# Routed expert tiles of a vision tower taken two at a time, with six weight buffers and the first four tiles' weights requested during routing

## The chip, the cores and the metric

One core of a Trainium2 chip runs the whole program. The metric is the time of one execution on the device in microseconds (us); of several executions the median counts. The engines are TensorE (PE, with its weight loads PEld), VectorE (DVE), ScalarE (ACT), GpSimd (POOL) and SyncE (SP, here an issuer of DMAs).

## What is computed

Sixty-four images become 1024 tokens of 192 values. Two layers follow: attention and a soft mixture of experts, then attention and a routed mixture of experts. The change lies in the last part, which is

```python
def _L1_ffn_ref(x, Wg, bg, Wge, bge, W1, b1, W2, b2):   # G=4 groups, E=8 experts each, D=192, M=768
    xf = x.reshape(-1, D)
    comb = _combine_weights(xf, Wg, bg, Wge, bge)       # best 2 groups, in each the best 2 experts
    h = jax.nn.gelu(jnp.einsum('nd,edm->nem', xf, W1) + b1, approximate=False)
    y = jnp.einsum('nem,emd->ned', h, W2) + b2
    out = jnp.einsum('ne,ned->nd', comb, y)
...
h = h + _L1_ffn_ref(_layernorm(h, axis=-1), L1_ffn_Wg, L1_ffn_bg, ...)
```

All arithmetic is fp32. Each token goes to 4 of 32 experts.

## The kernel before

`route` works out, for each of the 4096 (token, expert) pairs, a place in a list sorted by expert and padded so that every run of 128 places, a **tile**, has a single expert. There are `MOE_TILES` = 63 tiles. The tables are `rt.slot` (the token of every place) and `rt.expert` (the expert of every tile). The order in `route` is written out by hand: DVE computes the places, then one-hot matrices in four quarters; POOL multiplies them (L1325), PE sums them (L1350), and DVE turns the sums into `rt.slot` (L1448 to L1456) and last copies `rt.expert` (L1458). SP writes the normalised tokens to memory and waits for nothing but their landing.

`expert_tiles` then runs tiles 0 to 62. For tile t:

- POOL gathers the 128 token rows from memory into `x`, a ring of nine buffers (`gather`, L1717).
- SP reads the tile's expert from `rt.expert` and loads its two weight matrices, 576 KB each, into `w1` and `w2`, rings of three (`load`, L1521 and L1524). It waits until the hidden product (`hid_ready`), and then the output product (`y_ready`), of tile t-3 have left those buffers.
- PE transposes the 128 rows into the one bank `xp` (`transpose_x`, L1553); DVE copies them to `xT`, a ring of three, and picks the gate values (`leave_x`).
- PE makes the hidden values in `up`. The 192 input channels are split in 128 and 64. Six products over 128 rows (L1565) start the six chunks of 128 hidden values, and six products over 64 rows (L1568) end them. The even chunks' 64 rows lie on partitions 0 to 63 and the odd ones' on 64 to 127, so that two of them run in the array side by side. An fp32 product is two records in the trace, so the rows show 12 for six.
- ACT adds the bias and applies gelu (L1630) into `H`, a ring of three, as `hp` in PSUM is.
- PE makes the output in `down`: six products over 128 rows with 192 columns each (L1580) into the one bank `yp`. DVE scales them by the gate into `y`, a ring of three (`leave_y`, L1663), and POOL adds them to one of three sums in memory (`scatter`, L1729). `leave_y` of tile t waits until the scatter of tile t-3 has landed.

All engines follow the order that `tile` gives. On PE it is: transpose tile t+1, `up(t)`, `down(t-1)`. `program` writes out the first nine tiles and the last nine, and runs the 45 between in a loop of five rounds (`Fori`). The last two tiles aren't scattered; their rows are put in place by products (L1606). At the end SP reads the three sums back, DVE adds them, and SP writes the result.

## Time and profile before

| | us |
|---|---|
| median of 3 executions | 1133.21 |
| lowest, highest | 1131.98, 1136.58 |
| the profiled execution | 1137.21 |
| its span in the trace | 1135.4 |
| mean granted TensorE clock | 0.945 of full speed |

The page gives each engine's busy time, the span in 40 slices, the chain of work that ended last, and the costliest groups of instructions. PE is busy for 1011.5 us of the span (89%), ACT for 669.8, DVE for 396.8 and POOL for 256.9. The expert tiles run from 825 to 1123 us, so the last 300 us of the span are the part to read. PE's lengths in the timeline overlap, since a product starts before the one ahead of it has left the array; the distance between starts is what counts.

### The profile page before, as it was taken

What the parts mean: (1) busy time and instruction counts of PE and PEld (TensorE: products, weight loads), DVE (VectorE), ACT (ScalarE), POOL (GpSimd) and SP (SyncE); (2) the same over time, 40 slices, a digit from 0 to 9 for tenths busy, and PEclk for the clock granted to TensorE, in tenths of its full rate; (3) what the DMA queues carried; (4) which work ended last, traced back from release to release, by engine and by line L of the source; (5) the groups of instructions that cost most, each with busy time, mean ns of one, the idle gap of its engine ahead of it and who ended that gap; (6) DMA issues with size and microseconds to landing.
All of it is one profiled execution on the core that took longest, in us unless ns stands there. A gap on an engine that the chain in (4) does not pass through costs nothing. (4 is left out here: it accounts for less than half of the span.)

```text
span 1135.4 us, 22122 instructions
## 1 busy us (share of the span) xinstructions
PE 1011.5 (89%) x7464; PEld 659.8 (58%) x7464; DVE 396.8 (35%) x1021; ACT 669.8 (59%) x1227; POOL 256.9 (23%) x256
## 2 busy tenths in 40 slices
PE   8878779879999999999999998875179999999997
PEld 8345445433445444444444455454169999999996
DVE  2655968550011111111111114766932222222233
ACT  0475968579888888888888862361033343333431
POOL 0111333230000000000000000200455555555541
PEclk9889969889999999999999999897579999999999
DMA  9000008979555555445545501004089999999997
GB/s 345 15 1 1 1 30 334 317 301 175 124 126 115 124 125 117 113 112 116 127 101 124 123 1 47 0 1 134 1 316 311 312 306 307 314 306 305 315 287 198
DMA packets 76118, 185.27 MB, mean 163 GB/s; under 512 B 15889, under 2 KB 34545, under 8 KB 75769
## 3 DMA queue, kind: packets, MB, share of 16 engines
q1 hardware_dynamic: 63788, 169.45, 49.5%
q0 software_dynamic: 11808, 14.39, 6.4%
q8 instruction: 53, 0.87, 0.4%
q14 instruction: 37, 0.30, 0.1%
q10 hardware_dynamic: 432, 0.26, 0.1%
HBM read 148.37 MB, written 35.69 MB: 162 GB/s over the span
## 5 line engine op out<-in xcount | busy, mean ns | idle before, releaser
L1182 ACT ACTIVATE sle_H<-sle_hp 128x1024 f32<-128x1024 f32 x384 | 367.5, 1024 | 58.9 <-PE sle_hp L1119 58.8
L1630 ACT ACTIVATE ext_H<-ext_hp,ext_bias 128x128 f32<-128x128 f32 x378 | 104.2, 375 | 171.7 <-issue 154.7
L1136 PE MATMUL sle_up<-sle_H,sle_cw 128*32 128x512 f32 (+1 forms) x2048 | 192.6, 494 | 0.0
L1580 PE MATMUL ext_yp<-ext_w,ext_H 128*128 128x192 f32 x756 | 139.7, 335 | 0.6 <-issue 0.6
L1197 DVE STREAM_TRANSPOSE sle_UT<-sle_up 128x256 f32<-128x256 f32 x64 | 37.3, 583 | 292.9 <-PE sle_up L1136 292.9
L1580 PEld LDWEIGHTS ext_yp<-ext_w,ext_H 128*128 128x128 f32 x756 | 121.1, 190 | 8.4 <-issue 0.9
L1119 PE MATMUL sle_hp<-keep_G,keep_dT 99*128 99x512 bf16 (+1 forms) x512 | 102.4, 334 | 11.7 <-PEq L897 6.8
L1104 POOL COPY sle_cw<-keep_CT 128x128 f32 (+1 forms) x64 | 18.7, 293 | 394.2 <-PE sle_up L1136 394.1
L1136 PEld LDWEIGHTS sle_up<-sle_H,sle_cw 128*32 128x32 f32 x2048 | 53.7, 109 | 87.2 <-issue 73.8
L1119 PE MATMUL sle_hp<-sle_G,sle_dT 99*128 99x512 bf16 (+1 forms) x512 | 100.0, 327 | 1.1 <-ACT sle_H L1182 1.1
L1565 PE MATMUL ext_hp<-ext_xT,ext_w 128*128 128x128 f32 x756 | 95.9, 277 | 0.0
L1119 PEld LDWEIGHTS sle_hp<-keep_G,keep_dT 99*128 99x128 bf16 x512 | 45.0, 99 | 82.3 <-ACT sle_H L1182 32.8
L1565 PEld LDWEIGHTS ext_hp<-ext_xT,ext_w 128*128 128x128 f32 x756 | 90.7, 194 | 0.0
L1119 PEld LDWEIGHTS sle_hp<-sle_G,sle_dT 99*128 99x128 bf16 x512 | 44.5, 98 | 69.4 <-ACT sle_H L1182 30.3
L1641 DVE COPY ext_yi<-rmoe_slot 128x1 uint32 (+1 forms) x63 | 9.7, 154 | 204.1 <-PE ext_yp L1580 204.1
L1729 POOL DMA_INDIRECT sum<-ext_y,ext_yi x40 | 63.6, 1590 | 68.5 <-DVE ext_gate L1654 32.7
L1145 PE MATMUL sle_up<-keep_w,sle_UT 128*128 128x192 f32 x384 | 67.3, 326 | 0.8 <-DVE sle_UT L1197 0.8
L1717 POOL DMA_INDIRECT ext_x<-xn,ext_xi x63 | 62.0, 985 | 25.1 <-issue 18.3
L1145 PEld LDWEIGHTS sle_up<-keep_w,sle_UT 128*128 128x128 f32 x384 | 61.7, 190 | 2.1 <-DVE sle_UT L1197 1.7
L1568 PE MATMUL ext_hp<-ext_xT,ext_w 64*128 64x128 f32 x756 | 59.1, 289 | 0.0
L979 PE MATMUL hid_gps<-pre_w,vit_xnT 128*128 128x384 f32 x128 | 48.0, 520 | 5.4 <-DVE hid_rest L1022 5.4
L1568 PEld LDWEIGHTS ext_hp<-ext_xT,ext_w 64*128 64x128 f32 x756 | 47.1, 187 | 7.6
(272 smaller groups left out, 1206.9 us busy)
## 6 DMA issues: line engine op xcount, KB each, us to landing
ext_w<-W SPq DMA_DIRECT2D x126, 576.0 KB, 5.4
pieces<-hid_gp SPq DMA_DIRECT2D x16, 1152.0 KB, 4.6
keep_G<-pieces SPq DMA_DIRECT2D x32, 288.0 KB, 3.9
sle_G<-pieces SPq DMA_DIRECT2D x32, 288.0 KB, 3.8
pieces<-hid_gp SPq DMA_DIRECT2D x8, 768.0 KB, 5.3
keep_G<-pieces SPq DMA_DIRECT2D x32, 192.0 KB, 3.8
sle_G<-pieces SPq DMA_DIRECT2D x32, 192.0 KB, 3.8
keep_CT<-xT SPq DMA_DIRECT2D x6, 512.0 KB, 6.8
```

What stands on the lines that cost most here:

```text
L979: pe.matmul(gps[(STEPS * i + e) % 4][:, half, 0:HALF], g.wideT[:, 0, tokens], g.w1[:, e - 1, half * HALF:(half + 1) * HALF], start=True, s ...
L1119: mm = pe.matmul(hp[k % DEEP][:, j, off:off + width], dT[b][:, c * P:(c + 1) * P], G[b][:, (c // 2) * HID + at:(c // 2) * HID + at + width ...
L1136: mm = pe.matmul(to[32 * e:32 * e + 32], cw[:, p, 2 * e + grp, :], H[:, p, h:h + width], start=(p == 0 and grp == 0), stop=(p == 1 and grp ...
L1145: mm = pe.matmul(yps, UT[:, par, b, :], g.w2[:, b, :], start=(b == blocks[0]), stop=(b == blocks[-1]))
L1182: act.activation(H[:, p, WIDTH * k:WIDTH * (k + 1)], hp[k % DEEP][:].rearrange("p a c -> p (a c)"), ACT.Gelu_apprx_tanh).then_inc(gelu_don ...
L1197: dve.transpose(UT[:, par, at // 32:(at + width) // 32, 32 * j:32 * j + 32], src.rearrange("p (b c) -> p b c", c=32)).then_inc(ut_done[ban ...
L1565: pe.matmul(hp[q][:, c % 2, (c // 2) * P:(c // 2 + 1) * P], w1[:, q, c, :], xT[:, q, 0, :], start=(c < 2), stop=False)
L1568: mm = pe.matmul(hp[q][:, c % 2, (c // 2) * P:(c // 2 + 1) * P], w1[rows, q, HC + c // 2, :], xT[rows, q, 1, :], start=False, stop=(c >= H ...
L1580: mm = pe.matmul(yp[:, 0:D], H[:, q, c, :], w2[:, q, c, :], start=(c == 0), stop=(c == HC - 1))
L1630: act.activation(H[:, q, c, :], hp[q][:, c % 2, (c // 2) * P:(c // 2 + 1) * P], ACT.Gelu, bias=bias[:, q, c:c + 1]).then_inc(gelu_done, 1)
L1717: pool.indirect_dma_start(out=x[:, p, :], out_offset=None, in_=xn_dram, in_offset=bass.IndirectOffsetOnAxis(ap=xi[p][:], axis=0)).then_inc ...
L1729: pool.indirect_dma_start(out=sums[q], out_offset=bass.IndirectOffsetOnAxis(ap=yi[q][:], axis=0), in_=y[:, q, :], in_offset=None, compute_ ...
```

## The change

1. **Pairs.** `up` is cut in `heads` (the six 128-row products) and `tails` (the six 64-row products). Tile 0 runs by itself; tiles 1 to 62 run in 31 pairs. For a pair t, t+1 PE does: transpose t+1, `heads(t)`, `down(t-2)`, transpose t+2, `heads(t+1)`, `down(t-1)`, `tails(t)`, `tails(t+1)`. DVE and POOL follow that order.
2. **Six weight buffers.** `w1` and `w2` have six buffers (`DEPTH`), and the loads of tile t wait for tile t-6. The buffers and their semaphores now live in `routed_moe`, and are called `rmoe_w` in the listing. The other rings keep their depth, except the gate values (`GATES`), which have six.
3. **Weights during routing.** `rt.expert` is computed before the one-hot matrices instead of last, and SP requests the weights of tiles 0 to 3 (`AHEAD`) inside `route`. In `expert_tiles` SP writes `out` first, and then loads tile 4 and on.
4. **Straight code.** No engine has a loop any more; all 63 tiles are written out. The `turn` increments on POOL go away.

PE, in the second and third tile of the expert stage. Before:

```order
L1553 MATMUL ext_xp<-vit_ident,ext_x 128x128 x2
L1565 MATMUL ext_hp<-ext_xT,ext_w 128x128 x6
L1568 MATMUL ext_hp<-ext_xT,ext_w 128x128 x6
L1580 MATMUL ext_yp<-ext_w,ext_H 128x192 x6
L1553 MATMUL ext_xp<-vit_ident,ext_x 128x128 x2
L1565 MATMUL ext_hp<-ext_xT,ext_w 128x128 x6
L1568 MATMUL ext_hp<-ext_xT,ext_w 128x128 x6
L1580 MATMUL ext_yp<-ext_w,ext_H 128x192 x6
```

PE, one pair of the changed kernel (L1546 transposes, L1558 `heads`, L1576 `down`, L1564 `tails`):

```order
L1546 MATMUL ext_xp<-vit_ident,ext_x 128x128 x2
L1558 MATMUL ext_hp<-ext_xT,rmoe_w 128x128 x6
L1576 MATMUL ext_yp<-rmoe_w,ext_H 128x192 x6
L1546 MATMUL ext_xp<-vit_ident,ext_x 128x128 x2
L1558 MATMUL ext_hp<-ext_xT,rmoe_w 128x128 x6
L1576 MATMUL ext_yp<-rmoe_w,ext_H 128x192 x6
L1564 MATMUL ext_hp<-ext_xT,rmoe_w 128x128 x12
```

The same 64-row products stand in one run of twelve for two tiles, where two runs of six stood, each between products over 128 rows.

SP, at the end of routing. Before:

```order
L1312 DMA sum<-rte_zero 128x9x192 x2
L1314 DMA xn<-rmoe_gate 128x8x4
L1252 UNCONDITIONAL_BRANCH
L1514 UNCONDITIONAL_BRANCH
L1517 TENSOR_LOAD rmoe_expert
L1517 ISA x2
L1521 ISA
L1521 DMA ext_w<-W 128x1152
L1524 DMA ext_w<-W 128x1152
```

SP in the changed kernel, the first of four such loads:

```order
L1312 DMA sum<-rte_zero 128x9x192 x2
L1314 DMA xn<-rmoe_gate 128x8x4
L1469 TENSOR_LOAD rmoe_expert
L1469 ISA x2
L1472 ISA
L1472 DMA rmoe_w<-W 128x1152
L1475 DMA rmoe_w<-W 128x1152
```

The loads have moved ahead of the branch that ends `route`.

```diff
+            sp.wait_ge(rt.expert_ready, 1)
+            for t in range(rt.AHEAD):
+                load_weights(sp, a, rt, t)
...
+            dve.wait_ge(owner_out, 1)
+            dve.tensor_scalar(rt.expert[:], ps_cnt[0:1, P:P + MOE_TILES], float(EXPERTS - 1), None, ALU.min).then_inc(rt.expert_ready, 1)
...
-            dve.wait_ge(owner_out, 1)
-            dve.tensor_scalar(rt.expert[:], ps_cnt[0:1, P:P + MOE_TILES], float(EXPERTS - 1), None, ALU.min).then_inc(slot_done, 1)
-            dve.wait_ge(slot_done, 2)
+            dve.wait_ge(slot_done, 1)
+            dve.wait_ge(rt.expert_ready, 1)
+
+
+def load_weights(sp, a, rt, t):
+
+    q = t % rt.DEPTH
+    e = sp.value_load(rt.expert[0:1, t:t + 1], min_val=0, max_val=EXPERTS - 1)
+    if t >= rt.DEPTH:
+        sp.wait_ge(rt.hid_ready, t - rt.DEPTH + 1)
+    sp.dma_start(rt.w1[:, q].rearrange("p c n -> p (c n)"), a["W1"][bass.ds(e, 1)].rearrange("o p n -> (o p) n")).then_inc(rt.w1_in[q], 16)
+    if t >= rt.DEPTH:
+        sp.wait_ge(rt.y_ready, t - rt.DEPTH + 1)
+    sp.dma_start(rt.w2[:, q], a["W2"][bass.ds(e, 1)].rearrange("o p c n -> (o p) c n")).then_inc(rt.w2_in[q], 16)
...
-    DEEP, BODY, PLACED = 3, 9, 2
-    ROUNDS = MOE_TILES // BODY
+    RING, XS, GATES, PLACED = 3, 9, 6, 2
+    LAST = MOE_TILES - 1
+    PAIRED = range(1, LAST, 2)
...
+            sp.wait_ge(h_done, TILES // 2)
+            sp.dma_start(out[0:TOKENS].rearrange("(i p) d -> p i d", p=P), g.h[:]).then_inc(first_out, 16)
+            sp.dma_start(out[TOKENS:TOKENS + P], g.h[:, 0, :]).then_inc(first_out, 16)
+            for t in range(rt.AHEAD, MOE_TILES):
+                load_weights(sp, a, rt, t)
...
+            def heads(t):
+                q, w = t % RING, t % rt.DEPTH
+                pe.wait_ge(rt.w1_in[w], 16 * (t // rt.DEPTH) + 16)
                 pe.wait_ge(xT_done, t + 1)
-                if first and p == 1:
+                if t == 1:
                     pe.wait_ge(h_done, TILES // 2)
-                if not (first and p < DEEP):
-                    pe.wait_ge(gelu_done, HC * (t - DEEP + 1))
+                if t >= RING:
...
+            def tails(t):
...
-            def tile(t, p, r, first, last):
-                if first and p == 0:
-                    transpose_x(0, 0, 0)
-                if not (last and p == BODY - 1):
-                    transpose_x(t + 1, (p + 1) % BODY, r + (p + 1) // BODY)
-                up(t, p, r, first)
-                if not (first and p == 0):
-                    down(t - 1, (p - 1) % BODY, r + (p - 1) // BODY)
...
-            program(pe, tile)
-            down(MOE_TILES - 1, BODY - 1, ROUNDS - 1)
+            transpose_x(0)
+            transpose_x(1)
+            heads(0)
+            tails(0)
+            for t in PAIRED:
+                transpose_x(t + 1)
+                heads(t)
+                if t >= 2:
+                    down(t - 2)
+                if t + 2 < MOE_TILES:
+                    transpose_x(t + 2)
+                heads(t + 1)
+                down(t - 1)
+                tails(t)
+                tails(t + 1)
+            down(LAST - 1)
+            down(LAST)
...
+            def gather_index(t):
+                if t >= XS:
+                    dve.wait_ge(x_in[t % XS], 16 * (t // XS))
+                dve.tensor_copy(xi[t % XS][:], rt.slot[:, 0, t:t + 1]).then_inc(xi_ready, 1)
...
+                if t + XS < MOE_TILES:
+                    gather_index(t + XS)
...
-            program(dve, tile)
-            leave_y(MOE_TILES - 1, BODY - 1, ROUNDS - 1, False)
+            leave_x(0)
+            leave_x(1)
+            for t in PAIRED:
+                leave_x(t + 1)
+                if t >= 2:
+                    leave_y(t - 2)
+                if t + 2 < MOE_TILES:
+                    leave_x(t + 2)
+                leave_y(t - 1)
+                if t == LAST - 9:
+                    place_rows()
+                if t in (LAST - 7, LAST - 5):
+                    place_tile((t - LAST + 7) // 2)
+            leave_y(LAST - 1)
+            leave_y(LAST)
...
+            for t in range(XS + 2):
+                gather(t)
+            for t in PAIRED:
+                if t + 1 + XS < MOE_TILES:
+                    gather(t + 1 + XS)
+                if t >= 2:
+                    scatter(t - 2)
+                if t + 2 + XS < MOE_TILES:
+                    gather(t + 2 + XS)
+                if t - 1 < MOE_TILES - PLACED:
+                    scatter(t - 1)
+            pool.wait_ge(y_out[0], 16 * (MOE_TILES // RING))
...
+        rt.DEPTH, rt.AHEAD = 6, 4
...
+        rt.w1 = s.sb("w1", [P, rt.DEPTH, HC + HC // 2, P])
+        rt.w2 = s.sb("w2", [P, rt.DEPTH, HC, D])
+        rt.w1_in, rt.w2_in = ([s.sem(f"{n}{i}") for i in range(rt.DEPTH)] for n in ("w1_in", "w2_in"))
+        rt.expert_ready, rt.hid_ready, rt.y_ready = (s.sem(n) for n in ("expert_ready", "hid_ready", "y_ready"))
```

## Rows read from the trace of the kernel before

**Rows 1.** The page, costliest groups: shapes, count, busy us, mean ns, idle before:
```profile
L1565 PE MATMUL ext_hp<-ext_xT,ext_w 128*128 128x128 f32 x756 | 95.9, 277 | 0.0
```

**Rows 2.** Stretches: length, busy time of each engine, PEclk, DMA share, GB/s:
```profile
860.00:1088.68 228.68, 228.68 (x1902) 215.51 (x1901) 58.68 (x298) 87.56 (x350) 126.75 (x98) 1.00 0.99 309
```

**Rows 3.** Timeline of PE, one tile: start, length in us (merged instructions):
```profile
942.33 1.50 PE L1565 MATMUL ext_hp<-ext_xT,ext_w 128*128 128x128 f32 x12
943.76 0.94 PE L1568 MATMUL ext_hp<-ext_xT,ext_w 64*128 64x128 f32 x12
944.63 2.22 PE L1580 MATMUL ext_yp<-ext_w,ext_H 128*128 128x192 f32 x12
946.68 0.38 PE L1553 MATMUL ext_xp<-vit_ident,ext_x 128*128 128x128 f32 x2
```

**Rows 4.** Timeline of PE, single records around the two changes of shape:
```profile
943.56 0.28 PE L1565 MATMUL ext_hp<-ext_xT,ext_w 128*128 128x128 f32 x1
943.76 0.37 PE L1568 MATMUL ext_hp<-ext_xT,ext_w 64*128 64x128 f32 x1
...
944.42 0.28 PE L1568 MATMUL ext_hp<-ext_xT,ext_w 64*128 64x128 f32 x2
...
944.90 0.49 PE L1580 MATMUL ext_yp<-ext_w,ext_H 128*128 128x192 f32 x2
```

**Rows 5.** Timeline, other engines in the same tile:
```profile
944.80 1.66 ACT L1630 ACTIVATE ext_H<-ext_hp,ext_bias 128x128 f32<-128x128 f32 x6 [2.83 <-issue]
...
947.06 0.41 DVE L1663 TENSOR_SCALAR ext_y<-ext_yp,ext_gate 128x192 f32<-128x192 f32 x1
...
948.27 1.59 POOL L1729 DMA_INDIRECT sum<-ext_y,ext_yi  x1 [1.70 <-DVE ext_gate L1654]
```

**Rows 6.** Stretches of half a microsecond in the body, and the start:
```profile
942.00:942.50 0.50, 0.50 (x6) 0.48 (x5) 0.08 (x2) 0.00 (x0) 0.29 (x1) 1.00 0.56 230
...
833.40:836.00 2.60, 2.60 (x15) 2.48 (x14) 0.71 (x4) 0.00 (x0) 1.99 (x3) 0.54 1.02 417
```

**Rows 7.** DMA issues from 800 us on: count, KB each, median us to landing:
```profile
ext_w<-W SPq DMA_DIRECT2D x126, 576.0 KB, 5.4
ext_x<-xn,ext_xi POOLq DMA_INDIRECT x63, 5.3
...
sum<-ext_y,ext_yi POOLq DMA_INDIRECT x40, 6.0
```

**Rows 8.** Stretch in the middle of routing:
```profile
812.00:818.00 6.00, 2.00 (x16) 1.53 (x16) 6.00 (x4) 0.00 (x0) 6.00 (x5) 0.50 0.00 0
```

**Rows 9.** Timeline of the start of the expert tiles:
```profile
823.37 0.20 DVE L1458 TENSOR_SCALAR rmoe_expert<-rte_ps_cnt 1x63 int32<-1x63 f32 x1
...
825.08 0.37 SPq L1521 DMA_DIRECT2D ext_w<-W  x1
...
826.70 0.97 POOL L1717 DMA_INDIRECT ext_x<-xn,ext_xi  x1 [0.30 <-issue]
...
831.19 5.75 SPq L1528 DMA_DIRECT2D out<-vit_h  x1
...
833.40 2.65 PE L1565 MATMUL ext_hp<-ext_xT,ext_w 128*128 128x128 f32 x12
...
835.98 0.94 PE L1568 MATMUL ext_hp<-ext_xT,ext_w 64*128 64x128 f32 x12
```

**Rows 10.** Timeline at the end, the last two tiles' products:
```profile
1123.91 5.44 PE L1606 MATMUL ext_hp<-ext_y,ext_place 128*128 128x192 f32 x32 [0.66 <-DVE ext_y L1663]
```

**Rows 11.** Chain of waits at the end: start, length, what:
```profile
1117.40 3.47 DMA out<-ext_y,ext_yi
...
1121.39 6.78 DMA ext_third<-sum
```

**Rows 12.** Instruction packets in the straight part, 833 to 877 us:
```profile
q8 instruction: 3, 0.05, 0.4%
```

**Rows 13.** Chain in that part: start, length, what:
```profile
844.07 2.15 PE ext_yp L1580 x12
...
848.64 2.15 PE ext_yp L1580 x12
```

## What was predicted, and how

> **What bounds the kernel now.** I read four views in this order. The page's costliest groups show whether PE waits: its products of the expert tiles have next to no idle time ahead of them [rows 1]. The stretches say the same of the whole body: over 50 tiles, from 860 to 1088.68 us, PE is busy for the whole stretch at the full clock (1.00 of 2.4 GHz), ACT for 87.56 us, DVE for 58.68 and POOL for 126.75, while the DMA engines show a share of 0.99 at 309 GB/s [rows 2]. So a tile takes 228.68 / 50 = 4.574 us, PE sets it, and the DMA engines are the one other resource that is near full. The timeline gives the tile's parts by the distance between starts: `heads` 1.43 us, the 64-row products 0.87, `down` 2.05, the transposes of the next tile 0.22 (which is 4.574 less the three others) [rows 3].
>
> A busy PE is not PE at its peak, so the fourth view is single records. Heads follow each other at (943.56 - 942.33) / 11 = 0.112 us. The first 64-row product starts 0.20 us after the last head, 0.09 late; the six side-by-side pairs would take 6 x 0.112 = 0.67 us and take 0.87, 0.20 late; the products of `down` then follow at (946.68 - 944.90) / 11 = 0.162 us, twelve would take 1.94 and take 2.05, 0.11 late [rows 3, 4]. **Each entry into the 64-row shape and return from it costs 0.40 us of a tile's 4.574**, and nothing else on PE is lost.
>
> **The change part by part.**
>
> *Pairs.* Tiles 0 to 62 change shape and return 63 times before; now 32 times. What counts is the path to the end. The end hangs on the output of tile 60 (below), so I count up to the end of `down(60)`. Before, 62 entries lie ahead of it (tiles 0 to 61), after, 31 (tile 0 and 30 pairs): 31 x 0.40 = 12.4 us less. But `heads(62)` now stands ahead of `down(60)` (12 x 0.112 = 1.34 us more), and `tails(61)` behind it (0.67 less), which costs 0.7. Net gain 11.7 us. A pair then lasts 2 x 4.574 - 0.40 = 8.75 us.
>
> This holds if no new wait fills the time. Starting a pair at 0: transposes to 0.2, `heads(t)` to 1.6, `down(t-2)` to 3.5, transposes to 3.7, `heads(t+1)` to 5.1, `down(t-1)` to 7.0, both `tails` to 8.75. ACT needs 1.66 us for a tile's gelu and starts 0.17 after its products [rows 5]; `tails(t)` ends near 7.9, so gelu(t) ends at 9.8 and gelu(t+1) near 11.7, and `down(t)` starts at 10.3 (its first half needs only half of gelu(t)), `down(t+1)` at 13.8. DVE finishes scaling 0.79 us after `down` (947.06 + 0.41 - 946.68) [rows 3, 5], so `yp` is free at 4.3 for a `down` at 5.1: 0.8 us to spare, the tightest of the new distances. POOL issues two scatters (1.59 us each) and two gathers (1 us each) in 8.75. A scatter goes out at 4.5 and its buffer is wanted again three tiles on, at 8.75 + 7.0 = 15.8: 11.3 us for it.
>
> *The DMA engines* must move a tile in 4.38 us instead of 4.574, so 309 x 4.574 / 4.38 = 323 GB/s. A share of 0.99 over the body is an average in which shares over 1 fill dips: half a microsecond of the body shows 0.56 at 230 GB/s, and in the start, with a queue behind it, the share is 1.02 at 417 GB/s [rows 6]. I take it that they can do 323. The Trainium skill, "DMA: Bandwidth & Descriptors", section Specifications, gives about 358 GB/s as the limit of memory for one core; this case's 417 GB/s stands above it, so the measurement decides, and by either figure 323 fits.
>
> *Six weight buffers.* The median load lands 5.4 us after its issue and PE never waited for one [rows 1, 7], so by itself this is worth nothing. It is the cover for the pairs: each load goes out three tiles (13.1 us) earlier. Were the DMA engines held at the old 4.574 us a tile, they would fall behind by 0.2 us a tile, 59 x 0.2 = 11.8 us at the last, which this lead still hides.
>
> *Weights during routing.* In routing the DMA share is 0.00 and TensorE's clock at 0.50, its 1.2 GHz level [rows 8], so four tiles' weights (4.7 MB, some 12 us at 400 GB/s) land there unseen, requested near 806 us and needed from 831 on. SP does nothing else then. The copy of `rt.expert` (0.20 us [rows 9]) moves from the end of DVE's chain ahead of its one-hot work: up to 0.2 lost there, up to 0.2 won at the end; I take 0.1 lost, with 0.5 as the bound for anything that 4.7 MB of writes does to DVE and POOL. What it brings is at the start. PE's first heads start at 833.40, once the rows of tile 1, requested at 826.70, have landed 6.2 us later [rows 9], behind the loads of six weight matrices. The steady median of a gather is 5.3 [rows 7], and a scatter beside little traffic took 3.47 [rows 11]. So the gain lies between 0 and 2.7 us; without a queue ahead I take 4.4 us, a gain of 1.8. Part is lost again: the first heads took 2.65 us, and the 64-row products behind them 0.94, as everywhere in the body [rows 3, 9], so the clock rose near 835.9. If it rises at the same moment, those 64-row products run at half speed too, 0.9 us more; if it rises earlier, up to 1.3 more is won. I take 1.3 us gained (0 to 4).
>
> *Out written first.* `out` was requested behind six loads, with SP held for 5.75 us in its last issue [rows 9]; now it goes out some 1.3 us sooner on an empty queue, and the first scatter, which waits for it, is not late. It is hidden either way.
>
> *The end.* The last two tiles' placing products end at 1129.3 [rows 10], but the chain runs from tile 60's scatter (3.47 us) over the read of the third sum (6.78 us) to 1128.2 and then DVE's sums [rows 11]. After the change this chain starts from `down(60)` as before and keeps its length; PE's side ends no later against it (both `tails` 1.7 us, gelu of tile 61 hidden but for some 0.4, two `down`s), so nothing new is last.
>
> *Straight code.* The nine written-out tiles at the start ran without a gap: `down`s at 844.07 and 848.64, 4.57 us apart, as in the loop, while three packets of instructions were fetched [rows 12, 13]. The loop saves nothing and costs nothing on PE: 0.
>
> **Sum.** 11.7 + 1.3 - 0.1 = 12.9 us. The profiled execution took 1137.2 (span 1135.4, 1.8 around it), so it would become 1124.3. It stood 4.0 above the median of the runs; the gain is one of PE's clocked work and holds for the median too: 1133.2 - 12.9 = **1120.3 us**. Its own range, with the start's 0 to 4 and 0.3 us a pair for waits that I miss (30 x 0.3 = 9 at the most, half of it likely), is 1116.5 to 1125.
>
> **The rivals.**
>
> *The DMA engines are full after all.* For it: a share of 0.99 in the body, and the shares of two queues overlap, so that 0.56 in one half microsecond may be the exception. Against it: 417 GB/s at the start, and the lead. It bites only if the scatters (6.0 us median [rows 7]) behind a longer queue of weights need over 11.3 us. Then a pair goes back to 9.15 us, the 11.7 are lost and the start remains: 1133.2 - 1.2 = 1132. If it happens in part: 1125 to 1132.
>
> *The saving of a shape change is smaller than counted.* What I call late may be partly the first loads of a row of products, and come back where `heads` meets `down`, which now happens three times more in a pair. For it: the lateness is spread over four records. Against it: `down` to transposes to `heads` is passed without delay today. Half of it left: 1133.2 - 5.8 - 1.2 = 1126.
>
> *Instruction fetch stalls, slower.* Three blocks were fetched in 44 us on that queue [rows 12], one in 14.7 us, so the 206 us that were a loop need 14 more. If each held PE for a DMA's landing as the loads show it (5.4 us [rows 7]), that is 76 us, 1196; from 12.9 / 14 = 0.9 us a block the kernel is slower than before. Against it: the gapless start. The Trainium skill, "Runtime: NRT & Kernel Launch", section Instruction fetch mechanics, says that blocks are fetched ahead in sequence and that a taken branch is what can stall; by that rule straight code has no cost and the loop might have had one, which this trace doesn't show.
>
> *The early loads do nothing at the start* because a gather's landing is its own latency: that is the start's lower bound, 1121.6, inside my range.
>
> **How the numbers follow.** Forecast (1116.5 to 1125) 0.72; shape change worth half, or the DMA engines in part (1125 to 1130) 0.13; full DMA engines or another wait that takes it all (1130 to 1138) 0.07; slower by the fetch or a like stall 0.04; below 1116.5 (the start gives more) 0.04. For 8 in 10 the range goes from 1116 to 1128. A measurement of this kernel can tell some 0.5% from no change, 5.7 us, so faster is below 1127.5: 0.72 + 0.04 + 0.10 = 0.86; same 0.09; slower 0.05.
>
> **What would show it.** In the profile after: starts of the 64-row products in runs of 24 records, one run in 8.75 us; PE busy without a break at clock 1.00; DMA over 320 GB/s in the body; 4.7 MB moved between 806 and 820 us; first heads near 831.6. A gap ahead of `down` would point to ACT or DVE; gaps every 15 us to the fetch; loads landing ever later to the DMA engines; a `heads` after `down` that starts late to the shape rival.

## The result

| | median, us | lowest to highest | runs |
|---|---|---|---|
| before | 1134.52 | 1131.98 to 1139.70 | 10 |
| changed | 1127.03 | 1122.45 to 1130.78 | 10 |

The ratio is 0.993, with a 95% interval of 0.9906 to 0.9953: 7.5 us faster, where 12.9 were forecast. The median lies 6.7 us above the predicted point of 1120.3 and 2.0 above the forecast's own range (1116.5 to 1125); only the range for 8 in 10 (1116 to 1128) holds it. The profiled execution took 1124.8 us (span 1123.0), 12.4 us less than that of before, and this looks like the 12.9 that were forecast. It is not. Four parts of the trace, each between the same two events in both kernels:

| part | before | changed | difference |
|---|---|---|---|
| start of the program to the first one-hot comparison | 805.07 | 801.39 | -3.7, not touched by the change |
| to the expert stage's first product | 19.04 | 19.98 | +0.9 |
| to the first product of `down(0)` | 15.31 | 20.04 | +4.7 |
| to the end of the span | 295.9 | 281.6 | -14.3 |

So the change gave 8.7 us in this pair of executions; the other 3.7 came from code that it leaves alone. (The moved copy of `rt.expert` itself, 0.14 us ahead of the first comparison, falls in that first part.) Over the fourteen traces of this study the first part ends anywhere from 796.7 to 805.1 us, about as much as the runs of one kernel differ.

### The profile page after: what moved, and what is told of

Its sections match the earlier page's. It is cut to its first block and busy times, and to the rows that moved or that the text cites. A ratio compares the mean times of both kernels' runs of the same rounds, so it can differ in the third digit from the quotient of the medians.

```text
span 1123.0 us, 21359 instructions
## 1 busy us (share of the span) xinstructions
PE 996.8 (89%) x7464; PEld 653.3 (58%) x7464; DVE 390.0 (35%) x1021; ACT 666.5 (59%) x1226; POOL 257.4 (23%) x256
## 5 line engine op out<-in xcount | busy, mean ns | idle before, releaser
L1576 PE MATMUL ext_yp<-rmoe_w,ext_H 128*128 128x192 f32 x756 | 133.5, 326 | 1.1 <-issue 0.6
L1576 PEld LDWEIGHTS ext_yp<-rmoe_w,ext_H 128*128 128x128 f32 x756 | 121.6, 191 | 1.6 <-issue 1.6
L1558 PE MATMUL ext_hp<-ext_xT,rmoe_w 128*128 128x128 f32 x756 | 97.2, 280 | 0.0
L1558 PEld LDWEIGHTS ext_hp<-ext_xT,rmoe_w 128*128 128x128 f32 x756 | 91.9, 196 | 0.0
L1663 DVE COPY ext_yi<-rmoe_slot 128x1 uint32<-128x1 uint32 x63 | 9.7, 154 | 154.6 <-PE ext_yp L1576 152.2
L1564 PE MATMUL ext_hp<-ext_xT,rmoe_w 64*128 64x128 f32 x756 | 51.4, 283 | 0.0
L999 ACT ACTIVATE hid_gp<-hid_gps 128x768 bf16<-128x768 f32 (+1 forms) x40 | 34.0, 850 | 27.1 <-PE hid_gps L984 14.6
```

Source lines behind the costliest of these rows:

```text
L1558: pe.matmul(hp[q][:, c % 2, (c // 2) * P:(c // 2 + 1) * P], rt.w1[:, w, c, :], xT[:, q, 0, :], start=(c < 2), stop=False)
L1564: mm = pe.matmul(hp[q][:, c % 2, (c // 2) * P:(c // 2 + 1) * P], rt.w1[rows, w, HC + c // 2, :], xT[rows, q, 1, :], start=False, stop=(c > ...
L1576: mm = pe.matmul(yp[:, 0:D], H[:, q, c, :], rt.w2[:, w, c, :], start=(c == 0), stop=(c == HC - 1))
```

## The profile after

The body, in the view of stretches (length, busy time of PE, PEld, DVE, ACT, POOL, PEclk, DMA share, GB/s), beside [rows 2]:

```profile
860.00:1088.00 228.00, 228.00 (x1993) 218.23 (x1993) 61.00 (x312) 88.26 (x364) 129.42 (x100) 1.00 1.01 323
```

PE is busy without a break, as before, and the DMA engines move 323 GB/s instead of 309. One pair in PE's timeline, beside [rows 3]:

```profile
940.84 0.44 PE L1546 MATMUL ext_xp<-vit_ident,ext_x 128*128 128x128 f32 x2
941.12 1.50 PE L1558 MATMUL ext_hp<-ext_xT,rmoe_w 128*128 128x128 f32 x12
942.46 2.12 PE L1576 MATMUL ext_yp<-rmoe_w,ext_H 128*128 128x192 f32 x12
944.41 0.38 PE L1546 MATMUL ext_xp<-vit_ident,ext_x 128*128 128x128 f32 x2
944.63 1.50 PE L1558 MATMUL ext_hp<-ext_xT,rmoe_w 128*128 128x128 f32 x12
945.97 2.12 PE L1576 MATMUL ext_yp<-rmoe_w,ext_H 128*128 128x192 f32 x12
948.01 1.61 PE L1564 MATMUL ext_hp<-ext_xT,rmoe_w 64*128 64x128 f32 x24
949.55 0.44 PE L1546 MATMUL ext_xp<-vit_ident,ext_x 128*128 128x128 f32 x2
```

The pair lasts 949.55 - 940.84 = 8.71 us, where two tiles took 9.15. Its one entry into the 64-row shape shows as `down` 2.04 instead of 1.94 to 1.95, twenty-four records in 1.54 instead of 1.34, and 0.28 for the transposes behind them instead of 0.22: 0.09 + 0.20 + 0.06 = 0.35 us, where each tile of before paid 0.40.

What is new is at the start. The timeline of all engines, most lines left out:

```profile
827.23 2.77 PE L1558 MATMUL ext_hp<-ext_xT,rmoe_w 128*128 128x128 f32 x12
...
829.92 1.55 PE L1564 MATMUL ext_hp<-ext_xT,rmoe_w 64*128 64x128 f32 x12
...
831.40 0.44 PE L1546 MATMUL ext_xp<-vit_ident,ext_x 128*128 128x128 f32 x2
...
831.68 1.50 PE L1558 MATMUL ext_hp<-ext_xT,rmoe_w 128*128 128x128 f32 x12
...
834.86 0.95 POOL L1724 DMA_INDIRECT ext_x<-xn,ext_xi  x1 [0.30 <-issue]
837.83 0.42 DVE L1648 COPY ext_xT<-ext_xp 128x256 f32<-128x256 f32 x1 [9.61 <-remote]
837.83 1.28 ACT L1631 ACT_TABLE_LOAD   x1 [14.77 <-remote]
837.92 0.33 SPq L1472 DMA_DIRECT2D rmoe_w<-W  x1
...
838.40 0.66 PE L1546 MATMUL ext_xp<-vit_ident,ext_x 128*128 128x128 f32 x2 [5.22 <-DVE ext_xT L1648]
...
838.85 2.76 PE L1558 MATMUL ext_hp<-ext_xT,rmoe_w 128*128 128x128 f32 x12
```

The heads start 5.86 us after the stage's first product (9.29 before), a gain of 3.4. Then **PE stands still for 5.5 us**, from the last record of `heads(1)` at 832.9 to 838.40. It waits for DVE's copy of tile 2's transpose, and DVE waits for the semaphore of that transpose, which PE had issued at 831.40. ACT waits in the same way for the 64-row products of 829.92, and SyncE for the same semaphore. All three go on within 0.1 us of each other, at 837.8. Only GpSimd works meanwhile: gathers up to 835.8. The profile names no releaser ("remote"). But the trace also records each raise of a semaphore as an event of its own: that of the 64-row products, which belongs to the product that starts at 831.16, stands at 837.76, and that of the transpose (831.57) at 837.80. So it is not that an engine was late with work: what PE had raised reached nobody for 6 us. The clock rose at 831.2, with PE at work since 827.2, and fell back at 838.1, at the end of the gap, so the heads of 838.85 take 2.76 us again.

The routing, in the timelines of DVE and POOL, changed kernel:

```profile
801.25 0.21 DVE L1440 TENSOR_SCALAR rmoe_expert<-rte_ps_cnt 1x63 int32<-1x63 f32 x1
801.39 0.66 DVE L1445 TENSOR_TENSOR rte_in_tile<-rte_tile_lane,rte_tilef 128x504 f32<-128x504 f32 x1
801.98 1.20 DVE L1446 TENSOR_TENSOR rte_in_lane<-rte_lane,rte_lanef 128x1024 bf16<-128x1024 f32 x1
802.14 8.27 POOL L1328 TENSOR_TENSOR rte_row_in<-rte_in_tile,rte_row_tile 128x504 bf16<-128x504 f32 x1 [30.32 <-DVE rte_in_tile L1445]
...
803.71 1.21 DVE L1446 TENSOR_TENSOR rte_in_lane<-rte_lane,rte_lanef 128x1024 bf16<-128x1024 f32 x1
...
808.30 1.21 DVE L1449 TENSOR_TENSOR rte_work<-rte_mask,rmoe_gate 128x1024 f32<-128x1024 f32 x1
...
810.37 1.02 POOL L1328 TENSOR_TENSOR rte_row_in<-rte_in_tile,rte_row_lane 128x504 bf16<-128x504 f32 x1
...
817.46 1.00 PE L1353 MATMUL rte_ps_row<-rte_row_in,rte_in_lane 128*128 128x126 bf16 x8 [0.98 <-POOL rte_row_in L1328]
```

and before:

```profile
805.07 0.68 DVE L1440 TENSOR_TENSOR rte_in_tile<-rte_tile_lane,rte_tilef 128x504 f32<-128x504 f32 x1
...
805.84 1.94 POOL L1325 TENSOR_TENSOR rte_row_in<-rte_in_tile,rte_row_tile 128x504 bf16<-128x504 f32 x1 [29.47 <-DVE rte_in_tile L1440]
...
808.24 2.05 DVE L1441 TENSOR_TENSOR rte_in_lane<-rte_lane,rte_lanef 128x1024 bf16<-128x1024 f32 x1
...
820.07 1.00 PE L1350 MATMUL rte_ps_row<-rte_row_in,rte_in_lane 128*128 128x126 bf16 x8 [2.94 <-POOL rte_row_in L1325]
```

Before, DVE and POOL share the time, and both are slowed. Now DVE runs its eight comparisons and the product behind them at full pace (1.21 for 2.05 us), and POOL's first product lasts until DVE is through with them: 8.27 us for 1.94. It ends at 810.41, 0.9 us after DVE's product, and POOL's next one takes 1.02, so it got little or nothing before that. PE's last row sums start 16.07 us after the first comparison instead of 15.00.

## Experiments

All were timed against the kernel before on their own chip; three chips are told apart below as A, B and C. Four occasions of the changed kernel are on record; the chip of the first is not known, and each occasion has one trace.

### The changed kernel again

No edit.

> The changed kernel once more, for a second trace. Its first trace shows the body as forecast (a pair in 8.71 us), but PE standing still from 832.9 to 838.4 us in the first pair, because the first hidden product's semaphore came 6 us after its last product had started, and the first POOL product of routing taking 8.27 us where it took 1.94. Theory: both belong to the change (early loads, `out` written first) and recur in this trace at the same places; the run comes out 7 to 8 us under the kernel before, ratio 0.993. Rival: they were accidents of one execution; then this trace has neither, the first heads start 5.9 us after the stage's first product and nothing stands still after that, and the span is about 6 us shorter than 1123.

Measured: 1116.31 us, ratio 0.9835 (0.9794 to 0.9876), kernel before 1133.2: **16.9 us of gain instead of 7.5**. The standstill is gone, here with ACT's and DVE's next steps at once:

```profile
826.59 1.04 PE L1564 MATMUL ext_hp<-ext_xT,rmoe_w 64*128 64x128 f32 x12
...
827.73 1.28 ACT L1631 ACT_TABLE_LOAD   x1 [7.99 <-PE ext_hp L1564]
...
828.04 0.42 DVE L1648 COPY ext_xT<-ext_xp 128x256 f32<-128x256 f32 x1 [3.16 <-PE ext_xp L1546]
...
829.40 1.50 PE L1558 MATMUL ext_hp<-ext_xT,rmoe_w 128*128 128x128 f32 x12
```

POOL's 8.27 us product is there again. From the stage's first product to `down(0)` it is 12.69 us (20.04 in the first trace), from there to the end 281.5 (281.6). The body is the same to 0.1 us, and nearly the whole difference between the two traces within the stage, 7.4 of 7.5 us, is the standstill with the clock that it costs.

### Tile by tile

```diff
-                heads(t)
-                if t >= 2:
-                    down(t - 2)
...
-                tails(t)
-                tails(t + 1)
+                heads(t)
+                tails(t)
+                down(t - 1)
```

> The changed kernel with PE, DVE and POOL going tile by tile again (transpose t+1, heads t, tails t, down t-1); six buffers, early loads, `out` first and straight code stay. Theory (a change of shape and back costs 0.40 us): a tile takes 4.57 us again in the body, 31 x 0.40 - 0.7 = 11.7 us more than the changed kernel, so some 4 us slower than the kernel before (ratio 1.003) if the start loses what the changed kernel's start loses. Rival (the pairs gained less, the start gained): under 8 us more than the changed kernel. Straight code costs nothing: no gaps between tiles.

Measured: 1131.90 us, ratio 0.998 (0.9959 to 1.0), 15.6 us over e1_same beside it; 13.7 us between the two traces from the stage's first product to the end. A tile takes 4.574 us again. So **the pairs are nearly the whole gain**, and worth more than the 11.7 forecast.

### No weights during routing

```diff
-            sp.wait_ge(rt.expert_ready, 1)
-            for t in range(rt.AHEAD):
-                load_weights(sp, a, rt, t)
...
+            for t in range(3):
+                load_weights(sp, a, rt, t)
             sp.wait_ge(h_done, TILES // 2)
```

> The changed kernel with no weights requested in routing; tiles 0 to 2 are loaded at the start of the expert stage, ahead of `out`, as before; pairs, six buffers and straight code stay. Theory (early loads and `out` first bring the 5.5 us standstill and the slow POOL product): neither shows, POOL's products take 1.0 to 2.0 us, PE does not stop after its first heads, and the kernel is 11 to 12 us under the kernel before (ratio 0.990), some 4 us faster than the changed one. Rival (the standstill has another cause, or is an accident): it is 1 to 3 us slower than the changed kernel, by the gather that lands behind six loads again.

Measured: 1124.39 us, 8.1 over e1_same; 5.7 between the traces. `heads(0)` starts 9.15 us into the stage, as before the change (9.29), and later PE waits twice for weights, for instance:

```profile
844.46 1.60 PE L1557 MATMUL ext_hp<-ext_xT,rmoe_w 128*128 128x128 f32 x12 [1.46 <-DMA rmoe_w<-W]
```

POOL's long product (8.27 us) is there without a single weight being moved, so the early loads do not cause it. PE has no standstill here, but on this chip (A) the changed kernel had none either (e1_same), so the run says nothing of what the early loads do to it.

### Three buffers

```diff
-        rt.DEPTH, rt.AHEAD = 6, 4
+        rt.DEPTH, rt.AHEAD = 3, 3
```

> The changed kernel with three weight buffers instead of six and three tiles' weights requested in routing; pairs stay. Theory (six buffers are the cover of the pairs): the load of tile t+1 goes out at the start of a pair and is needed 3.7 us later, and lands after 5.4, so PE waits some 1.5 to 3 us a pair, 31 pairs: 45 to 90 us slower than the changed kernel, ratio 1.03 to 1.07. Rival (cover not needed): a pair still takes 8.71 us and the time is the changed kernel's.

Measured: 1171.32 us, ratio 1.033 (1.03 to 1.036), 55 us over e1_same (62.7 between the traces; the profiled execution was the slowest of the four). From the waits from 860 to 1088 us (engine, line, what for: us, times, longest):

```profile
PEld ext_hp L1558 <- DMA rmoe_w<-W: 40.7, 39, 2.6
```

With three buffers a pair frees both `w1` at its end and wants the first of them again some 4 us later, and a load takes 5.4 to land [rows 7]. Pairs without the deeper ring are slower than no pairs.

### The copy of rt.expert alone

```diff
             c.after(dve.tensor_copy(tilef[:], tilei[:]))
+            dve.wait_ge(owner_out, 1)
+            dve.tensor_scalar(rt.expert[:], ps_cnt[0:1, P:P + MOE_TILES], float(EXPERTS - 1), None, ALU.min).then_inc(slot_done, 1)
```

This is the kernel before, and the two lines are removed from the end of DVE's chain.

> The kernel before with one thing of the change: the copy of rt.expert stands ahead of the four pairs of one-hot comparisons. In every trace with the changed routing the first row_in product on GpSimd takes 8.27 us (1.94 before), the one-hot comparisons on VectorE 0.67 and 1.21 us (1.50 and 2.05 before), and the way from the first comparison to the expert stage's first product 19.98 us (19.04 before). Theory A (the order of the copy does it): all of that appears here, 1134 us, the way 20.0 us. Rival (it is where the tensors lie in SBUF, since w1 and w2 are now allocated ahead of the routing's): 1.94 us and 19.1 to 19.3 us as before. The time is 0.2 to 1.1 us over that before in either case, inside what the comparison resolves.

Measured: 1134.33 us beside 1135.02 for the kernel before, not to be told apart. But the trace is plain:

```profile
797.89 0.66 DVE L1442 TENSOR_TENSOR rte_in_tile<-rte_tile_lane,rte_tilef 128x504 f32<-128x504 f32 x1
...
798.63 8.27 POOL L1325 TENSOR_TENSOR rte_row_in<-rte_in_tile,rte_row_tile 128x504 bf16<-128x504 f32 x1 [27.64 <-DVE rte_in_tile L1442]
```

and 19.97 us to the stage's first product. **One 0.21 us copy in another place costs 0.9 us** on this way, by the order alone, far less than the times can resolve; where the buffers lie is ruled out. Why the order decides whether POOL or DVE has its way is not shown.

### The standstill: again, and with out later

e5_again is the changed kernel without an edit. The other edit:

```diff
-            sp.wait_ge(h_done, TILES // 2)
-            sp.dma_start(out[0:TOKENS].rearrange("(i p) d -> p i d", p=P), g.h[:]).then_inc(first_out, 16)
-            sp.dma_start(out[TOKENS:TOKENS + P], g.h[:, 0, :]).then_inc(first_out, 16)
             for t in range(rt.AHEAD, MOE_TILES):
                 load_weights(sp, a, rt, t)
+                if t == rt.DEPTH - 1:
+                    sp.wait_ge(h_done, TILES // 2)
+                    sp.dma_start(out[0:TOKENS].rearrange("(i p) d -> p i d", p=P), g.h[:]).then_inc(first_out, 16)
+                    sp.dma_start(out[TOKENS:TOKENS + P], g.h[:, 0, :]).then_inc(first_out, 16)
```

> The changed kernel a third time, unaltered. In the first comparison it took 1127.0 us with TensorE at a standstill of 5.49 us at 832.91 to 838.40 in its trace, in the second 1116.3 us without one, beside a kernel before of 1134.5 and 1133.2 us. Theory A (the standstill is an event of that comparison, not of the program): about 1116 us again, ratio 0.980 to 0.987, products from the first heads on without a gap of over 2 us. Rival (it comes in some share of executions of this program): times spread from 1110 to 1130 us with a gap of 5 us where the time is high.

> The changed kernel with the two writes of out issued behind the weights of tiles 4 and 5 instead of ahead of them. If the writes of out delay the first gathers and so the first products, the stage's start gets shorter by up to 1 us and the time lies 0 to 2 us under e5_again. If they do not, the time is the same. If first_out then comes late for the scatter of tile 0 (issued at 835.32 in the trace of the second comparison), GpSimd waits there and gathers behind it come later, but those have 9 tiles of lead: same time.

Measured, on one chip: 1126.82 us (ratio 0.9927, 0.9893 to 0.996) and 1122.99. The standstill is back, 5.55 us between the starts of records on either side, 828.30 and 833.85. With `out` later it is 1.80 us, but the gathers now queue behind 2.4 MB of weights, and PE is idle for 3.61 and 1.99 us ahead of its first two pairs of transposes (0.94 and 0.93 in e5_again). `down(0)` comes 19.0 us into the stage, for 20.2. It moved the delay more than it removed it; of the 3.8 us between the medians the traces show 1.2.

### Triples

PE's order for three tiles t to t+2, DVE and POOL alike:

```diff
+                transpose_x(t)
+                down(t - 4)
+                heads(t)
+                for n in range(2):
+                    transpose_x(t + n + 1)
+                    down(t + n - 3)
+                    heads(t + n + 1)
+                for n in range(3):
+                    tails(t + n)
```

> The changed kernel with the 64-row products of three tiles in one go: 21 entries into the 64-row shape instead of 32. Theory A (each entry with its return costs a fixed 0.40 us, and 0.44 by the difference of the tile-by-tile and the paired kernel, 13.8 us for 31): 11 fewer give 4.4 to 4.9 us, less up to 1 us at the end, where tile 60's rows are scattered later: 3.5 to 4.9 us under e5_again. A group then takes 13.1 to 12.9 us less 0.4, about 12.7 us. Rival (GELU of the third tile or its PSUM banks come late, as heads of the next group need the banks that the last GELUs free): gaps on TensorE of over 0.5 us per group, 21 of them, and a time 5 us or more over e5_again.

Measured: 1121.75 us, 5.1 under e5_again beside it. The two traces do not show that gain: from the stage's first product to the end they take 303.8 and 301.8 us, since triples win 3.0 from `down(0)` on and lose 5.1 ahead of it. (They are the slowest execution of triples and the fastest of e5_again.) A group takes 12.88 us (957.93 to 970.81 in PE's timeline), 4.295 a tile for 4.355, with no gap between:

```profile
957.93 2.28 PE L1564 MATMUL ext_hp<-ext_xT,rmoe_w 64*128 64x128 f32 x36
...
970.81 2.28 PE L1564 MATMUL ext_hp<-ext_xT,rmoe_w 64*128 64x128 f32 x36
```

Over 60 tiles that is 3.6 us, and 13.1 for pairs against single tiles (60 x 0.219). Two prices fit both: 0.40 for an entry and return as before [rows 4], and 0.35 for the one that a group keeps. A pair then saves 0.80 - 0.35 = 0.45 us (measured 9.15 - 8.71 = 0.44) and a group of three 1.20 - 0.35 = 0.85 (measured 3 x 4.574 - 12.88 = 0.84). The standstill takes another form here. PE's 64-row products, which wait for nothing, come one by one:

```profile
835.92 0.27 PE L1564 MATMUL ext_hp<-ext_xT,rmoe_w 64*128 64x128 f32 x1 [0.99 <-issue]
837.34 0.27 PE L1564 MATMUL ext_hp<-ext_xT,rmoe_w 64*128 64x128 f32 x1 [1.16 <-issue]
838.77 0.27 PE L1564 MATMUL ext_hp<-ext_xT,rmoe_w 64*128 64x128 f32 x1 [1.16 <-issue]
```

So PE's own issue is held as well, 1.43 us apart. SyncE's requests in the same stretch are at the same distance (834.44 and 835.88).

### Six tiles requested during routing, with pairs and with triples

```diff
-        rt.DEPTH, rt.AHEAD = 6, 4
+        rt.DEPTH, rt.AHEAD = 6, 6
```

> The changed kernel once more, unaltered, as the measure for the two kernels beside it. So far its time was 1127.0, 1116.3 and 1126.8 us, with a standstill of TensorE of 5.5 us in the traces of the first and the third comparison, none in that of the second. Theory A (in the stretch where the writes of out, the gathers and the weights of tiles 4 and 5 are all under way, the semaphores that TensorE raises can arrive 5 us late): 1116 or 1127 us, whichever the trace's gap behind the first heads goes with: 5.5 us of gap with 1127, none with 1116. Rival (the level belongs to the comparison, and the gap is chance): a trace whose gap does not go with the time.

> The changed kernel with the weights of six tiles requested during routing instead of four. 6.9 MB at the 386 to 420 GB/s seen there take 16.5 to 18 us, from 4 us behind the first comparison on, so they land about when the stage begins; behind the writes of out SyncE then waits for the first tile, and nothing of weights is under way beside the gathers. Theory A (the pile-up of transfers holds the semaphores): no gap behind the first heads, and a time at the level of 1116 us: as e9_fourth if that has no gap, 9 to 11 us under it if it has one. Rival (the transfers have nothing to do with it): the gap is there as often as in e9_fourth, and the time is the same. Against it could count that the last weights delay the first gathers: up to 3 us later first heads.

> Six tiles requested during routing, and the 64-row products of three tiles in one go. In e8_triples the body went with no gap but those of the start, where single 64-row products came 1.43 us apart, and the time was 5 us under e5_again. Theory A: the two gains add: 4 to 5 us under e10_six_ahead, about 1111 to 1112 us. Rival (triples only gained by moving the start): the same time as e10_six_ahead.

Measured, on another chip: 1124.95 us (ratio 0.9894, 0.985 to 0.9939), 1125.64 and 1124.79, not to be told apart. The unchanged kernel has a standstill of 6.00 us, the one with six tiles ahead 4.06, the one with triples six products 0.71 us apart. With six ahead, no weights are in flight, and the DMA engines are a third busy while PE stands (stretch, columns as above):

```profile
836.00:840.00 4.00, 0.97 (x9) 0.78 (x7) 0.00 (x0) 0.00 (x0) 2.84 (x3) 1.00 0.36 102
```

**So my theory of a pile-up of transfers falls**: neither the weights of tiles 4 and 5 nor full DMA engines are needed. With triples the way from `down(0)` to the end is 5.7 us shorter, but the way to it 7.0 longer (24.5 for 17.5): by its order one more tile's `heads` and two more tiles' `tails` stand ahead of `down(0)`, and they fall into the slow stretch at half the clock. So the body's gain is shown, the kernel's is not.

### Gathers paced

In four traces (the first, e5, e9, e10) ACT and DVE went on 0.7 to 2.2 us after the end of an unbroken train of eleven gathers on GpSimd. This breaks the train:

```diff
                 pool.wait_ge(xi_ready, t + 1)
+                if 3 <= t < XS:
+                    pool.wait_ge(xp_ready, min(t - 2, 4))
```

> The changed kernel with the first nine gathers of GpSimd paced: gather 3 and later ones wait for the transposition of tile 0, 1, 2 and from gather 6 on of tile 3, where they were issued one each 1.25 us without a pause. In four traces with a standstill (after, e5_again, e9_fourth, e10_six_ahead) TensorE goes on 0.8 to 2.3 us after a train of eleven gathers has ended, and the weights of tiles 4 and 5 are no part of the cause, since e10_six_ahead has the gap (4.06 us) without them. Theory A (the unbroken train of gathers holds up the semaphores that TensorE raises and SyncE's issues): the train breaks after five gathers, no gap over 1 us behind the first heads, the first down() 12.5 to 13.5 us after the stage's first product, as in e1_same (12.7) and e2_unpaired (13.0) and not 20 us as in e5_again, and a time of about 1116 us, 8 to 11 us under the 1125 to 1127 of the changed kernel. Rival (the writes of out hold them, and the train ends because of the standstill, not the other way): the gap stays at 4 to 6 us, and the time at 1124 to 1127 us. A train that is broken by its own waits could also shift the scatter of tile 0, which then costs up to 2 us at tile 3.

Measured: 1116.79 us, ratio 0.9853 (0.9811 to 0.9895), no standstill, `down(0)` 13.55 us into the stage. This is what the theory asked for, but the run fell on the chip of e1_same, where the changed kernel had no standstill either and took 1116.3. **It does not tell the theories apart.** And e1_same itself has a longer unbroken train, thirteen gathers from 818.78 to 835.01, without a standstill, so the train alone does not make one.

### All traces side by side

The stage is counted from its first product; "own form" is the slow issue of triples. The last column is the number of semaphore events that the trace holds from 6 to 16 us into the stage.

| chip | kernel | median, us | standstill, us | to `down(0)`, us | to the end, us | events |
|---|---|---|---|---|---|---|
| not known | before | 1134.5 | none | 15.3 | 311.3 | 216 |
| not known | changed (first) | 1127.0 | 5.49 | 20.0 | 301.6 | 37 |
| A | changed (e1) | 1116.3 | none | 12.7 | 294.2 | 184 |
| A | tile by tile (e2) | 1131.9 | none | 13.0 | 307.9 | 182 |
| A | no weights ahead (e3) | 1124.4 | none | 16.1 | 299.9 | 212 |
| A | three buffers (e4) | 1171.3 | none | 12.9 | 356.9 | 204 |
| A | paced (e12) | 1116.8 | none | 13.6 | 295.1 | 152 |
| B | changed (e5) | 1126.8 | 5.55 | 20.2 | 301.8 | 37 |
| B | before, copy moved (e6) | 1134.3 | 2.06 | 17.9 | 314.4 | 72 |
| B | out later (e7) | 1123.0 | 1.80 | 19.0 | 300.6 | 53 |
| B | triples (e8) | 1121.8 | own form | 25.2 | 303.8 | 33 |
| C | changed (e9) | 1125.0 | 6.00 | 20.1 | 302.9 | 34 |
| C | six ahead (e10) | 1125.6 | 4.06 | 17.5 | 300.4 | 31 |
| C | six ahead, triples (e11) | 1124.8 | own form | 24.5 | 301.7 | 31 |

No kernel with the change was free of it on chips B and C, and none had it on A. The kernel before took 1133.2 and 1133.8 on A, 1135.0 on B and 1135.4 on C. The old form loses on B too, by less: with only the copy moved (e6) ACT starts 2.2 us behind the first 64-row products (0.1 in e1_same), and `down(0)` comes 17.9 us into the stage, for 15.3 in the trace of before.

**The last column splits the traces as the standstill does.** Take the four traces of the one changed kernel. Up to the stage's first product each holds 10204 events; behind it e1_same holds 5306, and the first trace, e5 and e9 hold 3866, 3842 and 3919, with the same 21359 instructions in each. Events of landings are missing too, so that the view of the DMA issues from 800 to 1130 us gives a landing for the loads in e1_same (the last number) and none in the first trace:

```profile
rmoe_w<-W SPq DMA_DIRECT2D x124, 576.0 KB, 5.9
...
rmoe_w<-W SPq DMA_DIRECT2D x126, 576.0 KB
```

During the standstill the events that are left come in groups 0.7 us apart (833.5, 834.2, 834.9, 835.6, 836.3 and 837.0 in the first trace), and PE's slow products are two such steps apart in e8 (1.43) and one in e11 (0.71). So late semaphores and missing records go together in all traces; which of them makes the other, or what makes both, is not shown. That leaves a rival that no run here tests: that the recording of the events is what fills up and holds the engines. Every execution on record has a span and a granted clock, which come from a profile, so no time here is known without recording. Against it stands only that missing records by themselves cost nothing in the body: e6 lacks a third of the events that before has there (24 for 36 in 2 us), and from `down(0)` to `down(60)` both take 274.4 us.

## Why the prediction came out as it did

The point of 1120.3 was met on no level, and the first result falls between 1125 and 1130, where the prediction had put 0.13, for a saving of half the size or for DMA engines that are full in part. Neither happened. That the number still lies in the range for 8 in 10 is luck: without the standstill the gain was 16.1 us by the traces, over the 12.9 forecast, and the standstill took 7.4 of it. Nor do the bounds of 1116.5 and 1125 follow from their terms: a start of 4 us gives 1117.6, and a start of 0 with half of the 9 us of waits gives 1126.1.

- **Pairs, 11.7 us: right, and under-sized.** 12.4 for the entries is 13.3 by the traces (`down(0)` to `down(60)`: 274.4 us before, 261.1 in e5_again). The price of 0.09 + 0.20 + 0.11 = 0.40 [rows 4] was read rightly. What the sum missed is that the entry which stays in a pair is cheaper: the return cost 0.11 when `down` followed, and 0.06 now that the transposes do, so 0.35 is left and a pair saves 0.44 instead of 0.40. The 0.7 taken off for work moved ahead is there, as 0.8 us between the first heads and `down(0)` (6.84 in e1_same, 6.02 before).
- **DMA full: did not happen.** 323 GB/s, as worked out from [rows 2] (313 in e1_same), and 327 in triples, with PE never waiting in the body. "By itself worth nothing" holds for the six buffers (e2: 4.574 us a tile), and so does that they are the cover of the pairs: with three the pairs lose 55 us (e4).
- **The start, 1.3 us gained: the term was mis-sized, and the wait that decided was missing.** The heads came 3.4 us earlier, inside my 0 to 4. Without the early loads it is 0.1. Behind that, the standstill took 7.4 us (e1_same against the first trace), and it is in three of the four traces of this kernel. I had looked for new waits in the steady pair and for fetch stalls, never at what crosses between engines in the one stretch where all of them start at once. [Rows 9] may have held a sign of it: SyncE's issue of `out` was held for 5.75 us, about as long. Whether that is the same thing is not shown.
- **Routing, 0.1 us lost: 0.9.** I bounded it by 0.5 for what the loads' writes might do to DVE and POOL. They do nothing; moving the copy does. [Rows 8] showed DVE and POOL both busy for all of 6 us, which was a sign that each might be holding the other.
- **The end, 0: 1.1 us gained.** From the start of `down(60)` to the end it is 21.5 us before and 20.4 after. The read of the third sum takes 6.27 us instead of 6.78 [rows 11] in the first trace; most of the rest lies behind it (from its landing to the end of the span 6.88 for 7.23). Nothing in the change was aimed at either, and no run shows why.
- **Straight code, 0: right.** The page's instruction packets went from 53 to 64, PE has no gap in the body, and around the standstill, between the packets that start at 822.39 and 847.07 us, there is none. The fetch is ruled out as its cause. The Trainium skill, "Runtime: NRT & Kernel Launch", section Instruction fetch mechanics, says that the cost of going from one block of instructions to the next is mostly hidden; the trace agrees, with PE busy for 228.00 of the body's 228.00 us.
- **Fixed shape rival (half the saving): wrong**, by the same traces.

Summed without the standstill: 3.4 at the first heads, 0.8 lost to `down(0)`, 13.3, 1.1 and 0.9 lost in routing give 16.1 us, and 16.9 were measured. With 7.4 for the standstill it is 8.7, and 7.5, 8.2 and 10.4 were measured.

What stays open is the cause of the standstill: a path that semaphores, PE's issue and SyncE's requests have in common is a reading that fits all rows, but no run shows it, nor what fills it: the gathers, the writes of `out`, or the recording of the events. The paced kernel beside the unchanged one on chip B or C would test the gathers, and both kernels timed without a profile would test the recording. Until then the 7.4 us are shown as time that these executions took, not as time that the kernel takes when nobody records it.

## What to carry over

Count the changes of row shape on PE and group across tiles: each entry and return taken away saved 0.42 to 0.44 us here. In the body three in a group beat two by 0.06 us a tile; six weight buffers were enough for both, three were too few for pairs, and nothing between was run. Compare traces by stages between fixed events, since here 3.7 us of a 12.4 us difference came from code that nobody had touched. Where a stage starts with every engine issuing at once, run the kernel on more than one chip before believing the number. And count what a trace holds: where records are missing, the recording belongs among the suspects.

## What was unexpected in the hardware

- The same program took 1116 us on one chip and 1125 and 1127 on two others, while the kernel before differs by 2 us between them.
- Semaphores raised by PE arrived 6 us late at three engines at once, in the traces that lack four fifths of the semaphore events of that stretch (37 for 184).
- A product on GpSimd of 1.94 us took 8.27 while VectorE ran at full pace beside it, in all thirteen traces in which a 0.21 us copy stands ahead of VectorE's comparisons; in the one without it did not.
